# Causal attention block: TensorE work in 64-row tiles, PSUM as four equal places, new engine orders

## What is computed

```
q = (x @ Wq) ; k, v = split(x @ Wkv)            # 16 heads of 64
s = einsum('bhid,bhjd->bhij', q * 64**-0.5, k)
gm = max(s, axis=-1)                            # over the whole row, also masked keys
p = where(causal_mask, 0, exp(s - gm))
out = einsum('bhij,bhjd->bhid', p, v) / (sum(p) + 1e-8)
x = layernorm(x + out @ Wo + bo)
```

## Time and profile before

| | |
|---|---|
| median of 3 runs | 1086.66 us (1086.21 to 1087.02) |
| the profiled execution | 1084.1 us from first to last instruction; no other time is given for it |
| TensorE busy | 1033.0 us, 95% |
| VectorE, ScalarE, GpSimd busy | 915.7 (84%), 745.6 (69%), 582.8 (54%) us |

### The profile page before, as it was taken

One profiled execution on the slowest core, in us unless ns is written; L12 is line 12 of the kernel. 1 busy time (PEld: TensorE's weight loads), 2 busy tenths in 40 slices (PEclk: granted clock), 3 DMA queues, 4 the chain that ended last, 5 costly groups with the idle time before them and its releaser, 6 DMA issues. The chain is left out here.

```text
span 1084.1 us, 22071 instructions
## 1 busy us (share of the span) xinstructions
PE 1033.0 (95%) x7427; PEld 675.5 (62%) x7427; DVE 915.7 (84%) x1546; ACT 745.6 (69%) x1709; POOL 582.8 (54%) x918
## 2 busy tenths in 40 slices
PE   7899999999999999999999999999999999999895
PEld 5566666666666666666666666666666666666563
DVE  5988888988888888888889888888988888898967
ACT  5667667666676666676676667667666766766777
POOL 5355655555565455556555556655555565554364
PEclk9999999999999999999999999999999999999998
DMA  5255565445556545555654455565445556554542
GB/s 163 57 126 130 129 146 125 117 107 129 133 125 147 119 110 119 127 127 133 147 126 113 108 128 127 133 148 124 114 111 126 132 127 147 122 123 113 118 113 78
DMA packets 74209, 134.07 MB, mean 124 GB/s; under 512 B 26864, under 2 KB 36848, under 8 KB 74096
## 3 DMA queue, kind: packets, MB, share of 16 engines
q1 hardware_dynamic: 73520, 132.26, 51.6%
q10 hardware_dynamic: 576, 0.39, 0.2%
HBM read 21.17 MB, written 2.36 MB: 22 GB/s over the span
## 5 line engine op out<-in xcount | busy, mean ns | idle before, releaser
L746 DVE TENSOR_SCALAR_CACHE_REDUCE tile<-ps_s 128x1024 f32<-128x1024 f32 x512 | 608.5, 1222 | 137.7 <-PE ps_s L984 132.2
L576 ACT ACTIVATE tile<-tile,neg_max 128x640 f32<-128x640 f32 (+7 forms) x512 | 396.2, 774 | 206.7 <-POOL tile L407 206.4
L984 PE MATMUL ps_s<-ks,qs 64*128 64x512 f32 x3072 | 425.9, 409 | 6.0 <-DVE tile L746 4.0
L407 POOL TENSOR_SCALAR_AFFINE_SELECT tile<-tile 128x128 f32<-128x128 f32 x512 | 149.6, 293 | 449.3 <-DVE tile L746 446.9
L984 PEld LDWEIGHTS ps_s<-ks,qs 64*128 64x128 f32 x3072 | 269.7, 185 | 125.9 <-issue 61.7
L1038 PE MATMUL ps_x<-pt,vs 128*64 128x256 f32 (+1 forms) x2560 | 270.2, 361 | 1.1 <-issue 1.1
L755 DVE STREAM_TRANSPOSE stage<-tile 128x640 f32<-128x640 f32 (+3 forms) x256 | 255.2, 1025 | 0.0
L1038 PEld LDWEIGHTS ps_x<-pt,vs 128*64 128x64 f32 x2560 | 175.0, 137 | 107.9 <-issue 35.8
L997 PE MATMUL ps_x<-ident,tile 128*128 128x128 f32 x640 | 117.3, 290 | 22.6 <-ACT pt L624 11.9
L997 PEld LDWEIGHTS ps_x<-ident,tile 128*128 128x128 f32 x640 | 69.1, 140 | 103.2 <-issue 51.8
L918 PE MATMUL ps_x<-xs,ws 128*128 128x512 f32 x381 | 119.0, 421 | 0.1
(11 more groups left out here) (92 smaller groups left out, 576.7 us busy)
## 6 DMA issues: line engine op xcount, KB each, us to landing
pt<-stage SPq DMA_DIRECT2D x512, 120.0 KB, 2.5
pt<-stage SPq DMA_DIRECT2D x512, 88.0 KB, 2.1
rb<-recips SPq DMA_DIRECT2D x64, 256.0 KB, 4.1
y<-in_L_attn_x SPq DMA_DIRECT2D x3, 512.0 KB, 8.2
out<-y SPq DMA_DIRECT2D x3, 512.0 KB, 3.2
pt<-in_L_attn_Wkv SPq DMA_DIRECT2D x2, 384.0 KB, 6.7
pt<-in_L_attn_x SPq DMA_DIRECT2D x2, 256.0 KB, 4.6
wos<-in_L_attn_Wo SPq DMA_DIRECT2D x1, 512.0 KB, 7.2
```

Source lines behind the costliest of these rows:

```text
L407: pool.affine_select(out=block_of, in_=block_of, compare_op=ALU.is_ge, fill=fill, base=0, pattern=[[-1, P]], channel_multiplier=1).then_in ...
L576: act.activation(cols, cols, ACT.Exp, bias=neg_max[:, at:at + 1], scale=-1.0, accum_out=sums[:, p % 2, a, t:t + 1]).then_inc(s_exp, 1)
L746: dve.tensor_scalar(tile[:, at, :], ps_s[scores_at(p, t, a)][:, :], -SCALE, None, ALU.mult, ALU.min, accum_out=neg_max[:, at:at + 1]).then ...
L984: ins = mm(ps_s[scores_at(p, t, a)][:, c * HALF:(c + 1) * HALF], qs[rows, p % 2, qh, t * P:(t + 1) * P], ks[rows, p % 2, kh, c * HALF:(c + ...
```

## The change

All TensorE work of a turn except PV now uses 64-row tiles, the mode that S had already.

- Q and K: a contraction over 128 rows is cut in its lower and upper 64 rows. First the lower rows write columns 0 to 511 and the upper rows columns 512 to 1023 (two banks), then crosswise (`across`). Between the two halves TensorE waits on a semaphore of its own (`s_side`), since both then add to the bank that the other wrote. V and O are cut alike.
- T: two 64-row halves of each block, each 64 columns out, in three groups instead of seven units. ScalarE's three copies then read whole places.
- PSUM is four equal two-bank places (`NPLACES`), shared by all. Which user follows which in a place stands in a table (`FOLLOWS`).
- ScalarE copies q, k, v and O in one instruction of 1024 columns each (2 + 1 + 1 instead of 4 + 2 + 2). `ot` has two buffers.
- All engines have a new order. On TensorE Q, K and O stand together, and PV0 stands at the end of the turn behind PV2. On VectorE the turns of tiles 4 to 7 stand later. On SyncE the reciprocals stand behind all 16 moves of tiles 4, 5.

The core of the diff (the tables are cut, and so is what only follows from them):

```diff
-NSCORES = 3
-NSHARED = 2
+NPLACES = 4
+FOLLOWS = {
+    ("scores", 1, 0,): (("pv", 0,), 1),
+    ("scores", 3, 0,): (("group", 0,), 0),
+    ("scores", 6, 1,): (("group", 2,), 0),
+    ("q",): (("scores", 0, 0,), 1),
+    ("k",): (("scores", 0, 1,), 1),
+    ("group", 2,): (("v",), 0),
+    ("pv", 1,): (("scores", 5, 0,), -1),
...
-            def project_qk(p, what, c, bank, done):
-                for m, (wh, xh) in enumerate(terms):
-                    ins = mm(bank, ws[:, "qk".index(what), wh, r * P:(r + 1) * P],
-                             xs[:, b % XSLOTS, xh, c * HALF:(c + 1) * HALF], start=(m == 0), stop=(m == 2))
+            low, high = slice(0, DH), slice(DH, P)
+            across = (((low, 0), (high, 1)), ((high, 0), (low, 1)))
+            def project_qk(p, what, n):
...
+                else:
+                    pe.wait_ge(s_side[what], p)
+                for m, (wh, xh) in enumerate(terms):
+                    for rows, c in across[n]:
+                        cols = slice(c * HALF, (c + 1) * HALF)
+                        ins = mm(place[:, cols], ws[rows, "qk".index(what), wh, r * P:(r + 1) * P],
+                                 xs[rows, b % XSLOTS, xh, cols], start=(n == 0 and m == 0), stop=(n == 1 and m == 2))
+            def turn_group(p, g):
...
+                            for h, rows in enumerate((low, high)):
+                                out_cols = place[:, h * HALF:(h + 1) * HALF].rearrange("p (q c) -> p q c", q=2)
+                                ins = turn(out_cols[:, :, n * 32:n * 32 + 32],
+                                           tile[rows, slot_of(p, t, a), j * P:(j + 1) * P], ident[rows, rows])
```

More of the change, by code:

```diff
@@ L107 @@
[L107 to L112, removed]
+NPLACES = 4
+ORDER = [
+    ("scores", 0, 0, 0),
+    ("scores", 0, 1, 0),
+    ("scores", 1, 0, 0),
+    ("scores", 1, 1, 0),
+    ("q", -1),
+    ("k", -1),
+    ("out", 2),
+    ("scores", 2, 0, 0),
+    ("scores", 2, 1, 0),
+    ("group", 0, 0),
+    ("scores", 3, 0, 0),
+    ("scores", 3, 1, 0),
+    ("v", 0),
+    ("scores", 4, 0, 0),
+    ("scores", 4, 1, 0),
+    ("group", 1, 0),
+    ("group", 2, 0),
+    ("scores", 5, 0, 0),
+    ("scores", 5, 1, 0),
+    ("scores", 6, 0, 0),
+    ("scores", 6, 1, 0),
+    ("pv", 1, 1),
+    ("scores", 7, 0, 0),
+    ("scores", 7, 1, 0),
+    ("pv", 2, 1),
+    ("pv", 0, 0),
+]
@@ new lines, in is_real, with places_of_users @@
+def is_real(user):
+    kind, p = user[0:2]
+    return 1 <= p <= ALL_PAIRS if kind in ("q", "k") else 0 <= p < ALL_PAIRS
+def places_of_users():
+    place, before, users = {}, {}, []
+    fresh = 0
+    for k in range(-4, ALL_PAIRS):
+        for kind, *rest, back in ORDER:
+            user = (kind, k - back, *rest)
+            (kind2, *rest2), ago = FOLLOWS[(kind, *rest)]
+            past = (kind2, user[1] - ago, *rest2)
+            if past in place:
+                place[user] = place[past]
+                before[user] = past if is_real(past) else before.get(past)
+            else:
+                place[user] = fresh
+                fresh += 1
+            users.append(user)
+    assert fresh == NPLACES
+    first = [place["scores", 0, 0, 0], place["scores", 0, 0, 1]]
+    names = first + [n for n in range(NPLACES) if n not in first]
+    return {user: names.index(n) for user, n in place.items() if is_real(user)}, before, [u for u in users if is_real(u)]
@@ L216, in build @@
         s_turned = sem("s_turned")
-        s_quad = sem("s_quad")
+        s_group = sem("s_group")
+        s_side = {what: sem(f"s_side_{what}") for what in ("q", "k", "v", "out")}
         s_pt = sem("s_pt")
@@ L913, in _, with project_first @@
             pe.wait_ge(s_ident, 4)
[L915 removed]
+            def project_first(p, what, c, bank, done):
                 b, r = divmod(p, PAIRS)
@@ new lines, in turn_later_x, with project_out @@
+            def turn_later_x(b, c, bank):
+                pe.wait_ge(s_xraw[b], 16)
+                for t in range(4):
+                    ins = turn(bank[:, t * P:(t + 1) * P], x_raw[b][:, (4 * c + t) * P:(4 * c + t + 1) * P], ident[:, :])
+                ins.then_inc(s_xturned, 1)
+            def project_out(p, n):
+                place = places[PLACE.get(("out", p), SHARED)]
+                if n == 0:
+                    for c in range(2):
+                        pe.wait_ge(s_norm[c], p + 1)
+                    if p == 0:
+                        pe.wait_ge(s_wo, 16)
+                    if ("out", p) in PLACE:
+                        drained(("out", p))
+                    else:
+                        released(LAST_IN[SHARED])
+                else:
+                    pe.wait_ge(s_side["out"], p + 1)
+                for rows, c in across[n]:
+                    ins = mm(place[:, c * HALF:(c + 1) * HALF], wos[rows, p % PAIRS, :],
+                             ot[rows, p % 2, c * HALF:(c + 1) * HALF], start=(n == 0), stop=(n == 1))
+                ins.then_inc(s_side["out"] if n == 0 else s_out, 1)
```

754 lines of the change are left out of this document (453 added, 301 removed).

## The result

The changed kernel takes **1069.15 us** (median of 4 runs, 1067.7 to 1071.2) against 1086.54 for the kernel before on the same chip: ratio 0.984, 95% interval 0.9827 to 0.9854. It is 17.4 us faster; 1057 was forecast, with a range of 1040 to 1072. The profiled span is 1067.3 us, at a mean granted clock of 0.99.

The account below looks back on a forecast made before the run. TensorE's own stream was taken to set the turn: 27.6 us, 28.3 with self-waits, 30.2 with place waits and entries, 30.4 with SyncE's 0.2, against 31.42. Thus span 1054, median 1057 us, range 1040 to 1072.

Parts of the forecast that it names:

- the tail: Behind the turns: nothing shrinks, and exponentials (7, a) now standing behind PV0 in the last turn add 1 us.
- wait of PV2 of over 0.8 us in most turns: At PV2 near the turn's end: a sign that, if seen, would make the forecast wrong.
- rival 2: At PV2: moves of tiles 6, 7 land late, at 26.4 in most turns; turn 32.0, 1105 us; chance 0.15.
- the walk: One turn followed from S(0) through shared-place waits: waits 1.5 and new entries 0.36 on 28.3 give 30.2 us.
- The sum without waits, 27.6: TensorE's work per turn after the change: S 11.04, Q and K 2.76, V 1.39, T 2.2, O 1.72, PV 8.1.
- Overlap of the halves: TensorE's 64-row pairs in Q, K, V, T, O: taken whole, as in S; without any, 8 us more.
- Rival 3: Pieces of T, V, Q or K don't pair cleanly: 44 steps cost 1.1 us more, 1087 us; chance 0.13.
- An excursion at 0.35 to 0.4: TensorE leaving S's tile shape and returning: 0.35 to 0.4 us each, eight a turn before, two left after.
- Self-waits, 0.7 a turn: TensorE waiting on s_side between the halves of Q and of V: 0.35 us each.
- The wait ahead of group 2: T's group 2 waits 0.7 us for exponential (3, 1) on ScalarE, the costliest wait.
- SyncE, "+0.2": SyncE's last move lands at 24.0, PV2 wants it at 24.6; 0.2 us a turn added for late landings.
- Rival 1: The turn's forecast waits don't add: turn 29.0, 1012 us; chance 0.20.

Follow-up runs that it names:

- e11: Kernel of e7 with T, Q, K, V and O in 128-row tiles again and no self-waits on s_side: 1053.8 us, ratio 0.9698.
- e7: Changed kernel with PV0 ahead of PV2 at a turn's end, places exchanged and ScalarE's copies in the new order: 1033.9 us, ratio 0.9514.
- e10: Kernel of e7 with only T in 128-row tiles again: 1051.0 us, ratio 0.9671.
- e6: Kernel of e1 with Q, K, V and O in 128-row tiles again, without their self-waits: 1050.6 us, ratio 0.9671.
- e3: Changed kernel with two small DMAs more a turn in SyncE's queue behind the spreads: 1133.8 us, ratio 1.043.
- e1: Changed kernel with VectorE making the reciprocals behind eviction (0, 1), not behind (2, 0): 1044.7 us, ratio 0.9618.
- e2: Changed kernel with the three reciprocal DMAs of a turn (column and spreads) issued by ScalarE instead of SyncE: 1045.5 us, ratio 0.9621.

## Why the prediction was right in direction and off in size

The span was forecast at 1054 and came to 1067.3. The mean turn is 30.87 where 31.53 - 1.0 = 30.53 was forecast (10.5 us in 31 turns), and the tail gives back 4.2, not 1 (3.2 us): that is the whole miss, but for the 0.5 us by which the first S(0) came sooner.

By its own signs the forecast was wrong in mechanism and right in number. It named a wait of PV2 of over 0.8 us in most turns as such a sign, and 21 of 31 turns had it. What came is rival 2's place at a lower price. That 1069 lies in the range is in part luck: two errors of opposite sign, T too dear and SyncE's chain too short. With T's true price alone the walk would have reached PV2 some 0.5 sooner and forecast about 1041 (my estimate: turn 29.9).

- **The sum without waits, 27.6:** right for S (1.38 to 1.39), Q, K, V and PV. **T was mis-sized**: 0.11 a step from the 128-row rows, on the reason that loading 128 columns of weights sets it. The runs show 0.062 for a 64-row pair and 0.118 for a 128-row block (e11), so 20 steps are 1.24 us, not 2.2. Loading 128 columns can't set a step of 0.11, since each half of the pair loads 128 too; the reason given was wrong. The step halves where the columns that stream halve, though no run changed these without the rows.
- **Overlap of the halves:** as taken from S, for every kind. Rival 3 fell. By an estimate from the rule of the Trainium skill, "TensorEngine Tiling (Array Packing)", "Instruction Overhead", the 48 added instructions would cost 1.2 us a turn. The traces do not agree: Q's pair takes the 0.23 of S, T's pair 0.062 where one matmul took 0.118, and e11, without those instructions, is 20.0 us slower than e7.
- **An excursion at 0.35 to 0.4:** an entry or exit next to S shows 0.10 to 0.11 each side in e10 and e11 (S 1.49 instead of 1.38, 1.59 with both). Not all of an entry is the shape's: S(3) behind a wait in the same shape takes 1.46. What six excursions instead of two cost the whole turn in e11 was less than their sum: the wait ahead of group 2 took in 0.45, and the self-waits had gone.
- **Self-waits, 0.7 a turn:** Q's is seen, 1.03 us for three steps of 0.23. They eat what the edges of Q, K, V and O save (e6).
- **The walk:** right to 0.3 us at Q and group 2, up to 0.6 early later on. The wait ahead of group 2 (0.7, measured 0.81) is real, and the costliest of the walk; no run took it away alone.
- **SyncE, "+0.2":** this is the step that failed. The chain was put together rightly, and its parts were measured near: reciprocals 10.5 (10.7), last landing 24.9 (24.0), since 18 issues took 12.0 us and not 11.0. (By its own 0.63 they are 11.3, and the slack 0.3.) And the stream reaches PV2 at 24.1 and not 24.6: group 2 starts 0.3 sooner, its eight steps take 0.70 and not 0.88, and the wait of 0.2 ahead of PV1 did not come. Two errors of under a us, each small against the turn, turned a slack of 0.6 into a wait of 0.93, and 29.4 us over the kernel. A median was held against a median, with 0.6 between them, and the scatter priced at 0.2.
- **Rival 2** named the place and the mechanism, but the half clock behind a long wait was in no sum. The trace of the kernel before has it once: an S at 41.40 us takes 2.93 us instead of 1.66, behind a wait of 2.44. Two turns had it in the changed kernel (about 3.4 us); e3 shows what it does once the wait passes 2 us in most turns.
- **Rival 1 (waits don't add):** not refuted as to the walk's waits. The wait for the moves did add: taking it away gave 24 to 35 us.
- **The tail:** 4.2 us longer, and 1 was forecast. The low clock is a part that wasn't seen. The timelines of before and after, and of e7:

```profile
1026.03 1.12 PE L1049 MATMUL ps_x<-ot,wos 128*128 128x512 f32 x2 [2.14 <-POOL ot L415]
```

```profile
1005.33 4.21 PE L1214 MATMUL ps<-ot,wos 64*128 64x512 f32 x8 [3.01 <-POOL ot L495]
...
1005.33:1009.50 4.17, 4.11 (x9) 1.03 (x9) 4.00 (x22) 2.86 (x8) 0.00 (x0) 0.50 0.57 136
```

```profile
972.40 2.32 PE L1214 MATMUL ps<-ot,wos 64*128 64x512 f32 x8 [2.25 <-issue]
```

The idle stretch grew from 2.14 to 3.01 us, and O behind it ran at clock 0.50. Before, only one half of O stood here; now both do, in 8 matmuls. At full clock these take 2.32 us (e7), so of the 4.2 some 1.9 are the clock's and the rest is the work. But in e7, without that loss, the tail is still 95.8 us against 92.5 before. So the low clock isn't the main part of what the tail gives back; what is stays open.

## What to carry to other kernels

When a change makes the bounding engine faster, walk every other chain that feeds it to its last landing, and hold the slack against the scatter of that chain, not against its median: a slack of 0.6 us behind 18 queued DMAs was none here. The cheap repair is to put work that is ready in front of work that waits (e7, 35 us), before making the late chain shorter (e1, 24 us, since the moved instructions delayed something else). To know whether a DMA costs anything, add two of them: 65 us where the chain ended last, 0.7 where it did not.

## What the runs showed of the hardware

- Behind a wait of 2.0 us or more TensorE often runs on at half clock. In the changed kernel waits of 1.98 and 2.35 us did it, one of 2.29 us in the first turn did not, and waits up to 1.65 us never; in e3 a wait of 1.99 us had it and waits of 2.80 and 3.07 us had not, so the length of the wait alone doesn't decide. It costs PV2 and PV0 1.7 us in most cases, so a wait that grows by 1.2 us can cost 2.9.
- A block of T is transposed by a pair of 64-row matmuls in 0.062 us, and by one 128-row matmul in 0.118, although both load 128 columns of weights; 64 columns stream in the one and 128 in the other. Nothing in the trace of before showed that.
- A move that SyncE issues just behind two spreads of 256 KB on ScalarE's queue lands 5.8 us later in e2, against 2.3 in the changed kernel. Issuing sooner is not landing sooner.
- The step of a pair of 64-row matmuls with 512 columns is 0.23 us whether it is S, Q or K, so the pairing that S shows could be taken for Q and K.
